# An attention and 4-bit feed-forward layer on one core: 32 of 32 second products per pass summed by accumulating DMAs instead of 24 by GpSimd and 8 by VectorE

## What is computed

```
x = x + tanh(g_xattn[0]) * window_attention(_layernorm(x), ctx_4096, Wq, bq, Wk, bk, Wv, bv, Wo, bo)
# FFN on y = _layernorm(x); H = 1024, I = 3584, groups of 128 rows
gate_proj = (gate_w - gate_z) * gate_s        # 1024 x 3584, one scale per group and column
up_proj   = (up_w   - up_z)   * up_s
down_proj = (down_w - down_z) * down_s        # 3584 x 1024
x = x + tanh(g_ffn[0]) * ((silu(y @ gate_proj) * (y @ up_proj)) @ down_proj)
```

## Time and profile before

| | us |
|---|---|
| median of 3 runs (1656.76 to 1664.93) | 1661.05 |
| the profiled execution | 1667.74 |
| its span, first to last instruction | 1665.9 |
| PE, DVE, POOL, ACT busy in the span | 1574.3, 1517.5, 1452.7, 990.1 |

### The profile page before, as it was taken

One profiled execution on the slowest core, in us unless ns is written; L12 is line 12 of the kernel. 1 busy time (PEld: TensorE's weight loads), 2 busy tenths in 40 slices (PEclk: granted clock), 3 DMA queues, 4 the chain that ended last, 5 costly groups with the idle time before them and its releaser, 6 DMA issues.

```text
span 1665.9 us, 40474 instructions
## 1 busy us (share of the span) xinstructions
PE 1574.3 (95%) x16614; PEld 805.3 (48%) x16614; DVE 1517.5 (91%) x1483; ACT 990.1 (59%) x1133; POOL 1452.7 (87%) x891
## 2 busy tenths in 40 slices
PE   6898999897889999999999999999999999999996
PEld 3566667575533444444444444444444444444444
DVE  5687878776689999999999999999999999999997
ACT  4677778676445555555555555555555555555552
POOL 4576777676688999999999999999999999999975
PEclk9899999999899999999999999999999999999999
DMA  5655666655332222222222222222222222222128
GB/s 123 162 142 141 169 150 149 150 142 136 104 105 64 76 76 77 76 77 76 77 76 77 76 75 78 74 76 70 75 75 76 77 76 77 76 76 76 39 101 303
DMA packets 169522, 166.66 MB, mean 100 GB/s; under 512 B 11918, under 2 KB 135502, under 8 KB 169322
## 3 DMA queue, kind: packets, MB, share of 16 engines
q1 hardware_dynamic: 168186, 163.74, 34.9%
q10 hardware_dynamic: 1152, 0.33, 0.1%
HBM read 113.92 MB, written 16.78 MB: 78 GB/s over the span
## 4 chain that ended last, share of the span: by engine, by line
PE 84%; issue 5%; POOL 4%; DVE 3%; DMA 1%; ACT 1%; SPq 1%; ACTq 0%; DVEq 0%; POOLq 0%
PE bank L1168 63%; PE bank L1077 4%; PE bank L1066 3%; PE bank L1109 2%; POOL oacc L602 2%; DVE acc L950 2%; PE bank L1029 2%; PE bank L1040 2%; PE bank L1025 2%; PE bank L1033 2%; PE bank L1087 1%; PE bank L1056 1%; PE bank L1037 1%; PE bank L1045 1%; POOL raw_z L541 1%
## 5 line engine op out<-in xcount | busy, mean ns | idle before, releaser
L950 DVE SCALAR_TENSOR_TENSOR acc<-bank,scale,acc 128x1024 f32<-128x1024 f32 x784 | 950.5, 1272 | 13.7 <-PE bank L1168 8.9
L1168 PE MATMUL bank<-xT,w_int 128*128 128x512 f16 x3584 | 847.9, 380 | 13.2 <-ACT d_part L787 5.2
L602 POOL TENSOR_TENSOR oacc<-oacc,d_part 128x1024 f32<-128x1024 f32 x335 | 792.6, 2366 | 34.3 <-ACT d_part L787 19.1
L787 ACT ACTIVATE d_part<-bank,scale 128x1024 f32<-128x1024 f32 x335 | 372.7, 1113 | 379.9 <-PE bank L1168 373.3
L1168 PEld LDWEIGHTS bank<-xT,w_int 128*128 128x128 f16 x3584 | 349.5, 98 | 439.7 <-DVE acc L950 8.5
L1168 PE MATMUL bank<-h_hi,d_int 128*128 128x512 f16 x896 | 340.2, 380 | 9.0 <-ACT acc L767 2.5
L1168 PE MATMUL bank<-h_lo,d_int 128*128 128x512 f16 x896 | 339.5, 379 | 0.0
L541 POOL TENSOR_TENSOR raw_z<-raw_w,raw_z 128x512 int32<-128x512 int32 x168 | 264.1, 1573 | 9.0 <-DMA raw_z<-in_L_ffn_gate_z_dram 5.3
L1168 PEld LDWEIGHTS bank<-h_hi,d_int 128*128 128x128 f16 x896 | 87.4, 98 | 148.4 <-DVE acc L950 26.2
L974 DVE SCALAR_TENSOR_TENSOR oacc<-bank,scale,oacc 128x1024 f32<-128x1024 f32 x113 | 143.8, 1273 | 0.8 <-PE bank L1168 0.8
L668 ACT ACTIVATE pT<-bank 96x1024 f16<-96x1024 f16 x128 | 123.6, 1018 | 34.2 <-PE bank L1077 33.8
(11 more groups left out here) (84 smaller groups left out, 1377.2 us busy)
## 6 DMA issues: line engine op xcount, KB each, us to landing
raw_w<-in_L_ffn_gate_w_dram SPq DMA_DIRECT2D x56, 256.0 KB, 3.0
raw_z<-in_L_ffn_gate_z_dram SPq DMA_DIRECT2D x56, 256.0 KB, 3.7
raw_w<-in_L_ffn_up_w_dram SPq DMA_DIRECT2D x56, 256.0 KB, 3.0
raw_z<-in_L_ffn_up_z_dram SPq DMA_DIRECT2D x56, 256.0 KB, 3.7
raw_w<-in_L_ffn_down_w_dram SPq DMA_DIRECT2D x56, 256.0 KB, 2.7
raw_z<-in_L_ffn_down_z_dram SPq DMA_DIRECT2D x56, 256.0 KB, 3.4
vt<-vn_hl SPq DMA_DIRECT2D x64, 192.0 KB
vt<-vn_hl SPq DMA_DIRECT2D x64, 160.0 KB
```

Source lines behind the costliest of these rows:

```text
L602: nc.gpsimd.tensor_tensor(into, into, part, ALU.add).then_inc(d_added, 1)
L787: nc.scalar.activation(d_part[:, (count(c, x, False) - 1) % 2, :], pair[slot][:, :, :].rearrange("p h r -> p (h r)"), ACT.Copy, scale=scal ...
L950: nc.vector.scalar_tensor_tensor(out=into, in0=pair[u % 4][:, :, :].rearrange("p h r -> p (h r)"), scalar=scale[:, par, i, m, k:k + 1], in ...
L1168: last = nc.tensor.matmul(dst[:, h, :], weights, rows_of(h, part), start=(part == 0), stop=(part == 1))
```

## The change

Every down product but the four of `LATE_DVE` goes the first way, and the addition is a DMA issued by GpSimd with `accum_op=ALU.add`, SBUF to SBUF, 128 rows of 4 KB. `d_part` has four buffers (`NPART`) instead of two, and `d_added` becomes four semaphores, one for each buffer, which rise by 16 when that buffer's DMA has landed. GpSimd waits for the scaled buffer and for the landing of the DMA that last added to the same place of `oacc`; the wait for the addition just before is gone. ScalarE waits for the landing of the DMA four places back before it writes a buffer again. TensorE's last transposes wait for landings.

```diff
--- before.py
+++ after.py
@@ -49,9 +49,11 @@
     NCT = T // P
     LAG = NK + 3
 
+    NPART = 4
+
     FIRST_LATE = NQT * NK - LAG
     LATE_DVE = (FIRST_LATE + 2, FIRST_LATE + 5, FIRST_LATE + 9, FIRST_LATE + 10)
-    D_DVE = (2, 7)
+    D_DVE = ()
     XS = 256.0
     KH = NK // 2
     NGU = 4 * SC
@@ -161,6 +163,8 @@
         h_lo = sb("h_lo", [P, 2, TB], fp16)
         d_part = sb("d_part", [P, 2, TB], fp32)
         oacc = sb("oacc", [P, NCT, NT, TB], fp32)
+        d_more = sb("d_more", [P, NPART - 2, TB], fp32)
+        d_parts = [d_part[:, n, :] for n in range(2)] + [d_more[:, n, :] for n in range(NPART - 2)]
         row_dram = nc.dram_tensor("rows_after_attention", (B, P, T), fp32, kind="Internal").ap()
 
         pair = [ctx.enter_context(nc.psum_tensor(f"bank{n}", [P, 2, HALF], fp32)) for n in range(4)]
@@ -199,8 +203,9 @@
         unit_ready, acc_started, summed, silu_ready, hid_ready, h_hi_ready, h_lo_ready = (
             sem("unit_ready"), sem("acc_started"), sem("summed"), sem("silu_ready"), sem("hid_ready"),
             sem("h_hi_ready"), sem("h_lo_ready"))
-        down_ready, d_summed, d_scaled, d_added = (
-            sem("down_ready"), sem("d_summed"), sem("d_scaled"), sem("d_added"))
+        down_ready, d_summed, d_scaled = sem("down_ready"), sem("d_summed"), sem("d_scaled")
+
+        d_added = [sem(f"d_added{n}") for n in range(NPART)]
         row_back = [sem(f"rows_of_block{t}_back") for t in range(NT)]
         out_turned, out_ready = sem("out_turned"), sem("out_ready")
         stored, oacc_zeroed = sem("stored"), sem("oacc_zeroed")
@@ -278,6 +283,10 @@
 
         def by_dve(x):
             return (x + LAG) % NK in D_DVE
+
+        def d_landed(n):
+
+            return d_added[(n - 1) % NPART], 16 * ((n - 1) // NPART + 1)
 
         def taken_by_dve(c, x):
             return x in LATE_DVE if c == NC - 1 and x >= FIRST_LATE else by_dve(x)
@@ -590,16 +599,16 @@
             def add_down(c, x):
                 n = count(c, x, False)
                 pool.wait_ge(d_scaled, n)
-                if n > 1:
-                    pool.wait_ge(d_added, n - 1)
-                else:
+                if n == 1:
                     pool.wait_ge(oacc_zeroed, NCT)
                 cc, xx = ahead(c, x)
                 if cc >= 0 and taken_by_dve(cc, xx):
                     pool.wait_ge(d_summed, count(cc, xx, True))
-                part = d_part[:, (count(c, x, False) - 1) % 2, :]
+                elif cc >= 0:
+                    pool.wait_ge(*d_landed(count(cc, xx, False)))
+                part = d_parts[(n - 1) % NPART]
                 into = oacc[:, x % NCT, x // NCT // SC % NT, :]
-                nc.gpsimd.tensor_tensor(into, into, part, ALU.add).then_inc(d_added, 1)
+                nc.gpsimd.dma_start(into, part, accum_op=ALU.add).then_inc(d_landed(n)[0], 16)
 
             def zero_sums(tile):
                 if tile == 0:
@@ -753,7 +762,6 @@
             def take_scales(c, par):
                 if not isinstance(c, int) or c >= 2:
                     act.wait_ge(summed, (c - 1) * NQT * QS)
-                    act.wait_ge(d_summed, count(c - 1, -1, True))
                 nc.scalar.activation(scale[:, par], scales[:, bass.ds(c * SC, SC)], ACT.Copy).then_inc(scale_ready, 1)
 
             def start(c, u, par):
@@ -782,9 +790,9 @@
             def scale_down(c, x, par, slot):
                 n = count(c, x, False)
                 act.wait_ge(down_ready, c * NQT * NCT + x + 1)
-                if not isinstance(n, int) or n > 2:
-                    act.wait_ge(d_added, n - 2)
-                nc.scalar.activation(d_part[:, (count(c, x, False) - 1) % 2, :],
+                if n > NPART:
+                    act.wait_ge(*d_landed(n - NPART))
+                nc.scalar.activation(d_parts[(n - 1) % NPART],
                                      pair[slot][:, :, :].rearrange("p h r -> p (h r)"), ACT.Copy,
                                      scale=scale[:, par, x // NCT % SC, 2, x % NCT:x % NCT + 1])\
                     .then_inc(d_scaled, 1)
@@ -967,7 +975,7 @@
                     dve.wait_ge(oacc_zeroed, NCT)
                 cc, xx = ahead(c, x)
                 if cc >= 0 and not taken_by_dve(cc, xx):
-                    dve.wait_ge(d_added, count(cc, xx, False))
+                    dve.wait_ge(*d_landed(count(cc, xx, False)))
                 into = oacc[:, x % NCT, x // NCT // SC % NT, :]
                 src = pair[slot][:, :, :].rearrange("p h r -> p (h r)")
                 by = scale[:, par, x // NCT % SC, 2, x % NCT:x % NCT + 1]
@@ -1193,8 +1201,8 @@
 
                 if b == 0:
                     x = SC * NCT - 1
-                    pe.wait_ge(d_summed, count(NC - 1, x, True))
-                    pe.wait_ge(d_added, count(NC - 1, x, False))
+                    for n in range(NPART):
+                        pe.wait_ge(*d_landed(count(NC - 1, x, False) - n))
                 r = b * P
                 for ct_ in range(NCT):
                     last = nc.tensor.transpose(pair[slot][:, ct_ // 4, ct_ % 4 * P:(ct_ % 4 + 1) * P],
@@ -1204,7 +1212,10 @@
             def turn_col(ct_, slot):
 
                 x = NQT * NCT - NCT + ct_
-                pe.wait_ge(d_summed if x in LATE_DVE else d_added, count(NC - 1, x, x in LATE_DVE))
+                if x in LATE_DVE:
+                    pe.wait_ge(d_summed, count(NC - 1, x, True))
+                else:
+                    pe.wait_ge(*d_landed(count(NC - 1, x, False)))
                 for b in range(TT):
                     last = nc.tensor.transpose(pair[slot][:, b // 4, b % 4 * P:(b % 4 + 1) * P],
                                                oacc[:, ct_, 1, b * P:(b + 1) * P], ident[:, :])
```

## The result

The changed kernel takes 2003.77 us (median of 4 runs, 1998.12 to 2013.55) against 1660.3 us before (median of 4 runs): ratio 1.207, 95% interval 1.203 to 1.211. The forecast was 1848 us with a range to 2000. The direction was right and so was the new bound, the DMA engines; the size was short by nearly half: +343 us instead of +187.

A forecast was written before the change was run, and what follows sets the result against it. The prediction took VectorE, with TensorE right behind, to bound the kernel before, and the DMA engines after: 565 MB at 409 GB/s, 1382 us from 471 us, ends at 1853 us, adjusted to 1848 us; range 1643 to 2000.

The forecast's parts named there:

- What bounds before: Steady FFN: VectorE is last ready, costing 0.36 us of a 21.08 us quarter; TensorE's 20.72 us is the floor.
- VectorE and L957: VectorE per quarter: falls from 21.4 to 18.9 us, or 18.2 if L957 drops from 1.97 to 1.22 us.
- GpSimd's issue: GpSimd, eight DMA issues per quarter: 1 us taken for each, off the path if under 1.7 us.
- Rival 3: GpSimd bounds if an issue takes over 1.7 us; at 2.2 us a quarter is 24.5 us, total 1840 us; chance 0.04.
- Price of an accumulation: DMA engines, each 0.524 MB product: two passages at 409 GB/s, 2.56 us.
- Price of the loads: DMA engines, three weight pieces per quarter: 1.57 MB at 409 GB/s, 3.8 us.
- The sum: DMA work per quarter: 20.5 us products plus 3.8 us weights, 24.3 us against TensorE's 20.72.
- rival 2: Single transfers land late, so L787 waits once or twice a quarter: about 1755 us, or 1703 with half; chance 0.10.
- The waits for late loads: ScalarE's late landings would stop TensorE; GpSimd's own wait, 20.7 us old, costs nothing as long as DMAs keep pace.
- The end: Last column, DMA engines already full (0.98) between 1628 and 1664 us: seven late accumulations there can't hide.
- The signs named for the profile after: FFN: DMA share near 1.0, about 400 GB/s or half, L787 waiting for DMAs, down products over 3 us apart, DVE 75 to 80%.

The follow-up runs named there:

- e7: Changed kernel, but five of eight down products by accumulating DMA (three buffers), three by GpSimd's addition; last 11 as in the kernel before: 1645.97 us, ratio 0.992.
- e3: Changed kernel, but VectorE keeps two down products of eight and six go by accumulating DMA: 1679.75 us, ratio 1.012.
- e9: Kernel before, but the seven of the last 11 products that GpSimd adds go by accumulating DMA: 1684.57 us, ratio 1.013.
- e6: Changed kernel, but four of eight products by accumulating DMA (two buffers), three by GpSimd's addition, one by VectorE; last 11 as before: 1652.46 us, ratio 0.995.
- after: The changed kernel itself, as shown by its profile, with all but the four LATE_DVE products by accumulating DMA: 2003.77 us, ratio 1.207.
- e2: Changed kernel, but from pass 1 on each load of a weight piece moves a quarter of its bytes: 1730.37 us, ratio 1.043.
- e5: Changed kernel, but three slots for weight pieces instead of two, so each load is issued a piece earlier: 1913.38 us, ratio 1.152.
- e8: As e3, but GpSimd's addition replaces DMA in the last 11 products, and the DMAs have three buffers instead of four: 1664.09 us, ratio 1.0005.
- e1: Changed kernel, but GpSimd's DMAs copy into oacc instead of adding, so the sums are left out: 1649.0 us, ratio 0.994.

## Why the prediction came out as it did

- **What bounds before.** Right. TensorE's floor of 20.72 us per quarter and VectorE's stall of 0.36 us over it: in e7, without a down product on VectorE, 145 issues at five a quarter are 29 quarters in 600 us, 20.7 us each. The gain that was to be had was 1%, and there was no room for more; e7 got 0.8%.
- **VectorE and L957.** Right. Its median fell from 1.97 to 1.22 us where GpSimd adds nothing (e3, 1.215), and stayed at 2.12 in e9, where it does. In e6 and e7, with three additions of eight on GpSimd, it was 1.23, so it depends on what runs beside it. The rule of the Trainium skill's "SBUF — State Buffer" (Who interferes with whom), that a VectorE instruction with two SBUF inputs contends with a GpSimd instruction that reads SBUF, agrees in e3 and e9.
- **GpSimd's issue.** 1 us was taken, 0.93 to 0.98 measured. Rival 3 is out.
- **Price of an accumulation.** Two passages at 1.28 us, 2.56 forecast; 2.72 measured (after), 2.74 in e3 (54.7% of 1677.9 us for 335). +0.16 us, 1.2 us a quarter. The copy cost 1.43, and the addition made it 1.90 times as dear. The factor of the Trainium skill's "Collectives: The Full Stack" (The bandwidth ceiling: the fold count and why AG ≠ RS ≠ AR), 1.93, would make 2.76 us of the copy, an estimate; it was taken on collectives, and the measured factor of 1.90 agrees with it. Where the engines weren't full the price was higher, not lower: 2.88 us in e6 and 2.83 in e7 (54.7% and 68.1% of 600 us for 114 and 144.5 transfers).
- **Price of the loads: the term that was mis-sized most.** The prediction put their 1.57 MB per quarter at the rate of the end's stores, 409 GB/s, 3.8 us. Their own row stood in the same table: 0.25 share for 76 GB/s is 304 GB/s, 5.2 us; in after 19.8% of 600 us for 22 quarters is 5.4. It used that rate for the upper bound of the accumulations and not for the loads, to which it belongs. +1.6 us a quarter.
- **The sum.** 24.3 us forecast; with the measured prices 21.7 + 5.4 = 27.1, and measured 27.3. (The rise of 3.3 us in the prediction should read 24.3 - 21.08 = 3.2, and rival 2's 85 us are 52 x 1.6 = 83; neither moves the forecast.) That fits too well, for two things cancel: the engines reach a share of 1.04 to 1.07 (e2, e3, e5), so 27.1 is worked off in some 25.5 us (e5: 94 + 95 issues are 23.6 quarters in 600 us, 25.4 us each), and the bubble takes the rest back.
- **The waits for late loads: the step that was left out.** The prediction named what is queued behind ScalarE's waits for landings and said that GpSimd's own wait, for a landing, costs nothing. It was an old wait that began to cost: L550 in front of a late load, with the accumulations behind it on GpSimd, and the cast that needs L550 in front of the emptying of the PSUM pairs on ScalarE. Slower loads were in the sum as engine time, but not as lateness. e5 shows what this was worth: 90 us. With most of it gone the changed kernel is at 1913 us, inside the range.
- **The end.** Seven accumulations that can't hide: right, 18.6 us in e9 (14.8 against e8's end), and 61.6 us (2002.6 - 1941.0, the last start of L965, its L957) instead of 35.2 for after's end.
- **The signs named for the profile after.** DMA share near 1.0 (0.99), 209 GB/s as about half of 400, L795 waiting for DMAs and down products over 3 us apart (27.3/8 = 3.4) all came; VectorE was busy for 67%, less than the 75 to 80% of a shorter quarter.
- **Account in full**: 336.7 us between the spans. The end takes 26.4; the rest, 310 us, is 6.0 us for each of the 52 quarters, of which 3.2 were in the forecast.

## What to carry to other kernels

Before work goes from a compute engine to the DMA engines, add up the DMA time per period, with each kind of transfer at the share that its own rows show, and an accumulation at about twice a copy: here six in eight fitted (1.04 of the engines) and eight didn't, and the difference was 324 us. Where a queue gets full, every other user of it gets late, so look for every engine that waits for those, directly or through another engine, and for what stands behind that wait in its list: here the accumulations on GpSimd and the emptying of PSUM on ScalarE. And leave the stretches in which stores fill the DMA engines to the compute engines.

## What the runs showed of the hardware

- An accumulating DMA of 128 x 4 KB, SBUF to SBUF, took all 16 DMA engines for 2.72 us, a copy by the same queue 1.43 us, with the same packets and bytes in the profile. The byte columns don't show what the addition costs: after moved 209 GB/s at 0.99, e1 278 at 0.81. GpSimd was busy for 0.93 to 0.98 us in the mean with the issue of an accumulation (after), and for 0.53 to 0.55 us with that of a copy (e1).
- Summed over the queues the DMA share goes over 1: 1.04 to 1.07 held for 600 us in e2, e3 and e5. The 0.99 of after is therefore a mean over full stretches and bubbles.
- TensorE's granted clock fell to 0.50 (1.2 GHz) while it stood still for 5.3 us, and stayed there for about 5 us after it had started again (6 matmuls in 2 us against 10); in 600 us of after the mean was 0.92, in e5 0.96. That is a second price of each bubble, and it is within the 90 us of e5.
